# Opening of a pairwise-interaction kernel: gathers, weight preparation and w2 loads in another order, x_pairs in 42 rows a shift

## The reference

```python
h = inputs = e
for i, (W, bias) in enumerate(params):            # W: (200, 1600), (200, 4000), (200, 4000)
    x = einsum('bhd,bmd->bhmd', h, inputs).reshape(B, -1, D)
    y = relu(einsum('oi,bid->bod', W, x) + bias[None, :, None])
    if i != n_layers - 1:
        h, direct = split(y, 2, axis=1)           # 100 maps go on, 100 are output
    else:
        direct = y
    outs.append(direct)
z = concatenate(outs, axis=1).sum(-1)             # (512, 400)
h = concatenate([z, dense_ctx], axis=1)
h = maximum(h @ W_top1 + b_top1, 0.0)
h = maximum(h @ W_top2 + b_top2, 0.0)
y = h @ W_top3
```

## Time and profile before

| | us |
|---|---|
| median of 3 executions (lowest to highest) | 2825.09 (2822.59 to 2827.53) |
| profiled execution, its own time | 2823.11 |
| its span in the profile | 2821.3 |
| TensorE busy (matmul) | 2776.4, 98% |
| VectorE busy | 2637.5, 93% |
| ScalarE busy | 1499.5, 53% |
| GpSimd busy | 851.2, 30% |
| mean granted TensorE clock | 0.997 of full |

### The profile page before, as it was taken

The page is one execution under the profiler, slowest core; times in us unless marked ns, Lnnn a source line. Parts: engine busy times, 40 slices in busy tenths (PEclk is TensorE's granted clock), DMA queues, the critical chain, the costliest instruction groups (busy, mean ns, idle before and its releaser), DMA issues.

```text
span 2821.3 us, 54078 instructions
## 1 busy us (share of the span) xinstructions
PE 2776.4 (98%) x19032; PEld 2760.6 (98%) x19032; DVE 2637.5 (93%) x1945; ACT 1499.5 (53%) x1880; POOL 851.2 (30%) x700
## 2 busy tenths in 40 slices
PE   5899999999999999999999999999999999999999
PEld 5899999999999999999999999999999999999997
DVE  6899999999999999999999999999999999999995
ACT  4555555555555555555555555555555555555553
POOL 5432332332332332323323323323323323333100
PEclk9999999999999999999999999999999999999999
DMA  7333433433433433433334334334334334333330
GB/s 210 85 80 81 93 89 78 96 89 76 101 85 78 98 86 83 95 84 87 92 80 94 88 76 98 89 75 102 85 79 99 85 82 96 84 86 94 85 78 18
DMA packets 286024, 249.66 MB, mean 88 GB/s; under 512 B 31285, under 2 KB 284445, under 8 KB 285892
## 3 DMA queue, kind: packets, MB, share of 16 engines
q1 hardware_dynamic: 216310, 200.56, 25.8%
q0 software_dynamic: 65712, 45.56, 12.3%
q10 hardware_dynamic: 3972, 3.17, 0.4%
HBM read 140.74 MB, written 4.20 MB: 51 GB/s over the span
## 4 chain that ended last, share of the span: by engine, by line
PE 94%; SPq 2%; DMA 1%; issue 1%; POOL 1%; DVE 1%; another core or an unknown queue 0%; ACT 0%; DVEq 0%; ACTq 0%
PE acc L806 62%; PE acc L808 29%; PE hid_ps L819 1%; PE z_ps L823 1%; POOL gathered L445 1%; SPq L380 1%; PE acc L877 0%; DVE product L713 0%; DVE tails L718 0%; SPq L347 0%; SPq L369 0%; DMA hid_rep<-hid 0%; DMA gathered<-in_table,rows_all 0%; PE hid_ps L900 0%
## 5 line engine op out<-in xcount | busy, mean ns | idle before, releaser
L806 PE MATMUL acc<-weights,heads 126*128 126x400 f32 (+1 forms) x9088 | 2690.6, 364 | 12.1 <-DVE tails L718 12.1
L808 PE MATMUL acc<-weights,tails 126*128 126x200 f32 (+1 forms) x9088 | 2320.5, 255 | 0.0
L519 ACT ACTIVATE heads<-product 126x1024 fp32r<-126x1024 f32 (+2 forms) x1152 | 1198.2, 1047 | 1019.9 <-PE acc L808 509.5
L808 PEld LDWEIGHTS acc<-weights,tails 126*128 126x128 f32 (+1 forms) x9088 | 1739.3, 191 | 0.0
L806 PEld LDWEIGHTS acc<-weights,heads 126*128 126x128 f32 (+1 forms) x9088 | 1711.4, 188 | 14.1 <-issue 8.8
L718 DVE TENSOR_TENSOR tails<-product,heads 126x1024 fp32r<-126x1024 f32 (+2 forms) x1152 | 1347.9, 1202 | 1.4 <-ACT heads L519 1.4
L713 DVE TENSOR_TENSOR product<-hid_rep,x_rep 126x2048 f32<-126x2048 f32 x510 | 1166.9, 2288 | 107.1 <-PE acc L808 67.3
L453 POOL DMA_DIRECT2D acc_copy<-acc_copy x189 | 235.0, 1243 | 1726.0 <-ACT acc_copy L525 1724.0
L445 POOL DMA_INDIRECT gathered<-in_table,rows_all x320 | 503.6, 1574 | 101.2 <-issue 97.2
L533 ACT ACTIVATE y_relu<-acc_copy 128x400 f32<-128x400 f32 x192 | 102.4, 533 | 216.6 <-DMA acc_copy<-acc_copy 214.3
L525 ACT ACTIVATE acc_copy<-acc 128x800 f32<-128x800 f32 x192 | 158.6, 826 | 12.7 <-PE acc L808 5.8
(11 more groups left out here) (26 smaller groups left out, 118.1 us busy)
## 6 DMA issues: line engine op xcount, KB each, us to landing
x_rep<-x_rows SPq DMA_DIRECT2D x512, 120.0 KB
hid_rep<-hid SPq DMA_DIRECT2D x511, 120.0 KB
x_pairs<-x_rows SPq DMA_DIRECT2D x191, 280.0 KB
acc_copy<-acc_copy POOLq DMA_DIRECT2D x189, 200.0 KB
hid_rep<-hid SPq DMA_DIRECT2D x511, 5.0 KB
x_pairs<-x_rows SPq DMA_DIRECT2D x63, 120.0 KB
gathered<-in_table,rows_all POOLq DMA_INDIRECT x320
raw_weights<-in_w SPq DMA_DIRECT2D x8, 500.0 KB, 7.4
```

The source lines that it names most:

```text
L519: act.activation(heads[0:rows, ring % HEADS_RING, 0:tiles, :], product[0:rows, ring % PRODUCT_RING, 0:tiles, :], ACT.Copy).then_inc(heads_ ...
L806: nc.tensor.matmul(acc[:, at.parity, c, 0:2 * LAYER], dims(heads[0:rows, ring % HEADS_RING, k, :], c), w, start=(q == 0 and k == 0), stop= ...
L808: last = nc.tensor.matmul(acc[:, at.parity, c, LAYER:2 * LAYER], dims(tails[0:rows, ring % PRODUCT_RING, k, :], c), w[:, 0:LAYER], start=F ...
```

## The change

- `x_pairs` holds 42 rows for each shift where it held 40, so its product part has 126 rows (`ROWS0`), and the row of ones moves from partition 120 to 126. The two rows more hold products with zero weights. All x_pairs loads have 42 or 126 rows.
- VectorE waits for a marker that GpSimd writes after block 0's five gathers, before it adds w0b to w0a.
- The first two chunks of w1 are split ahead of w0. `split_place` maps a chunk to its place in that order, for the waits.
- SP loads the first half of block 0's x_rep right behind block 0's x_pairs, ahead of block 1's x_pairs. The last three chunks of w1, which stood there, go behind block 1's x_pairs. The second half of x_rep goes behind block 0's maps.
- SP loads w2 behind block 1's maps for layer 1, where it stood ahead of them. Its chunks are split three in layer 1 and four in layer 2 of iteration 2, where five were split in layer 0 and 1 up to q = 2 and none in layer 2.
- GpSimd: block 0's repeated maps of group 1 are issued between the stores of blocks 2 and 3, not behind both; block 5's first gather goes ahead of the wait and the `add` before it.
- 4 identity matmuls in place of 9, twice.

```diff
+FIELDS_PADDED = 42
+ROWS0 = SHIFTS * FIELDS_PADDED
-OPERAND_ROWS = (PAIRS0 + 1, PAIRS + 1, PAIRS + 1)
+OPERAND_ROWS = (ROWS0 + 1, PAIRS + 1, PAIRS + 1)
-BUSY = 9
+BUSY = 4
...
             if i == "start":
-                return list(range(split_until[0])) + w1[:4]
+                return w1[:2] + list(range(split_until[0])) + w1[2:4]
             if (i, layer) == (0, 0):
                 return w1[4:]
-            if (i, layer) == (2, 0):
-                return w2[:3]
-            if (i, layer) == (2, 1):
-                return w2[3 + q // 2:4 + q // 2]
+            if (i, layer) == (2, 1) and q > 0:
+                return w2[q // 2 - 1:q // 2]
+            if (i, layer) == (2, 2) and q < GROUPS - 2:
+                return w2[(3, 4, 5)[q // 2]:(4, 5, 7)[q // 2]]
             return []
...
-                parts.append((x_pairs[j:PAIRS0:SHIFTS, 1:1 + TILES0, :],
+                parts.append((x_pairs[j:ROWS0:SHIFTS, 1:1 + TILES0, :],
                               bass.AP(tensor=rows.tensor, offset=rows.offset,
-                                      ap=[[COLS, FIELDS], [SHIFTS * COLS, TILES0], [1, COLS]])))
+                                      ap=[[COLS, FIELDS_PADDED], [SHIFTS * COLS, TILES0], [1, COLS]])))
...
         def _(sp):
-            load_weights(EARLY_LOADS, split_until[1])
+            load_x_rep(0, 0, 0)
             sp.wait_ge(prep_added, 2)
...
                 if not whole and i == 0:
-                    load_x_rep(0, 0, 0)
-                    load_x_rep(0, 0, 1)
+                    load_weights(EARLY_LOADS, split_until[1])
                 if not whole and 0 < i < blocks and l2 is None:
                     for half in range(FLD_HALVES):
                         load_x_rep(duo, parity, half)
-                    load_weights(split_until[1], split_until[2])
...
                     load_hid(0, (0, 2, 3) if not whole and i == 0 else range(HID_OUT))
+                    if not whole and i == 0:
+                        load_x_rep(0, 0, 1)
+                    if not whole and i == 1:
+                        load_weights(split_until[1], split_until[2])
...
         def _(pool):
+                if b == 0:
+                    pool.memset(marker[:, blocks - 1:blocks], 0.0).then_inc(first_rows_asked, 1)
             for b in range(2, FIRST):
                 pool.wait_ge(first_gathered[b], GATHERS)
                 for part in stored_parts(b, b):
                     pool.dma_start(*part).then_inc(first_stored[b], 16)
+                if b == 2:
+                    pool.wait_ge(hid_copied[0], 1)
+                    for part in hid_parts(0, 1):
+                        pool.dma_start(*part).then_inc(hid_first_loaded, 16)
             add(0)
-            pool.wait_ge(hid_copied[0], 1)
-            for part in hid_parts(0, 1):
-                pool.dma_start(*part).then_inc(hid_first_loaded, 16)
...
                 first = 1 + (b - FIRST) * 3
+                ahead = 1 if b == FIRST + 1 else 0
+                for k in range(ahead):
+                    gather(0, k, rows_all[:, b, k:k + 1], x_gathered)
                 add(first)
-                for k in range(FLD_DMA):
+                for k in range(ahead, FLD_DMA):
                     gather(0, k, rows_all[:, b, k:k + 1], x_gathered)
...
         def _(dve):
+            dve.wait_ge(first_rows_asked, 1)
             for n in range(2):
                 dve.wait_ge(prep_loaded[n], 16)
```

23 lines of the change are left out of this document (15 added, 8 removed).

## The result

| | before | after |
|---|---|---|
| median us (runs; lowest to highest) | 2824.6 (22; 2820.9 to 2827.5) | 2828.1 (22; 2826.2 to 2833.9) |
| ratio of the times, 95% interval | | 1.0017 [1.0011, 1.0022] |
| profiled execution, its own time; span | 2823.11; 2821.3 | 2828.56; 2826.8 |
| mean granted clock | 0.997 | 0.996 |

The change costs 0.17%, some 4.8 us by the ratio; by its interval 3.1 to 6.2 (the two medians are 3.5 us apart). 2818.5 was forecast, in 2813.5 to 2825.5: wrong in sign, and outside the range.

A forecast was written before the change was run, and what follows sets the result against it. TensorE, busy for 2776.4 of 2821.3 us, was taken to bound the kernel, with VectorE setting the opening's pace. Terms of -1.1 (w2's tails) and -4.5 (the long gather) took 2824.1 to 2818.5 us, range 2813.5 to 2825.5.

The forecast's parts named there:

- Step 1: Start to block 0's x_pairs: closer gathers save 1.5 us, 42 rows 1.2; block 0's product starts at about 22.7.
- Step 2: w1's load issued 7.1 us later: block 0's accumulator copy +1.7, first layer 1 product +2.0; bounds 0 and +2.9.
- Step 3: w2's loads behind block 1's maps: maps asked for at 64.9, block 1's first layer 1 product at 70.0, -2.4.
- Step 4: w2's tails come later, where VectorE has no hole: +3.3, a closed hole -0.76; TensorE becomes level, -1.1 us.
- Step 5: Block 5's first gather, 11.19 us, issued at about 88 within GpSimd's wait: -4.5 us, bounds 0 and -4.9.
- Rival B: The long gather is not hidden, another behind the same add takes it: 2823.0 us, chance 0.16.
- Step 6: Rows 121 to 127, identity matmuls 9 to 4 twice, block 0's maps on GpSimd and padding: at no cost.
- Rival D: Cold TensorE: with 4 identity matmuls layer 0 of two blocks runs at half clock; 2823.3 us, chance 0.05.
- Rival C: Slower: the long time falls on the add behind the hoisted gather; 2827.4 us, or 2831.9; chance 0.07.

The follow-up runs named there:

- the experiment: The changed kernel with w1's last three loads issued ahead of the first half of x_rep, where they stood before: 2820.17 us, ratio 0.9999 to before.
- the kernel with four memsets: After with w1's load early, five w2 loads waiting for the add, ScalarE's w2 heads one turn earlier, a memset behind each block 0 layer 2 product: 2816.45, 0.9976.
- the kernels with the memset in its place and later: Before plus a one-element VectorE memset, behind block 0's layer 2 product of groups 6 and 7 (2816.79, 0.9974) or behind block 3's layer 0 product (2820.51, 0.9997).

## Why the prediction was wrong, point by point

**Step 1, start to x_pairs.** Product at 24.31, not 22.7. Block 0's gathers did take 0.94 us each but for the first two (1.19 and 1.00), but the x_pairs were asked for 0.9 us earlier and not 1.5. The 42 rows were taken at 1.2 us, near the upper bound; alone they gave 0.12 in one pair of executions, and some 0.5 over all. The Trainium skill (DMA: Bandwidth & Descriptors, "Why a DMA increments its semaphore by 16 and not by 1") would make 1.4 us of it, as the prediction estimated from its rule. The DMA share rises as the rule has it, the time does not fall by as much; why is not shown.

**Step 2, w1's late load. The step that made the change slower.** SP's issue came 6.9 us later, 7.1 was predicted (the five x_rep DMAs took SP 3.8 us, as reckoned, though five times the 0.8 named there are 4.0). But two sizes were off. Behind nine loads from x_rows the weights took 6.1 us to arrive (32.20 to 38.28) where 3.7 had done (25.31 to 29.02): so the last heads came 9.8 us later and not 6.5 to 7.1. And 36.89 was taken as the baseline, which is the late copy of one execution; with the load early the copy is at 34.89. What the step gave as +1.7 to +2.0 was +4.9 against before and +6.9 against what the rest of the change would have had. Its upper bound of 2.9 came from the issue time alone, with no bound for what the load takes from issue to arrival there. In the sum it was worse: the +2.0 was set against VectorE's later gains in step 3 and got no price of its own. By the experiment it is the whole loss against before.

**Step 3, w2's loads behind the maps.** Right. For block 1's first layer 1 product -2.4 was predicted and +0.93 measured (73.31). But the -2.4 held the +2.0 of step 2, so it was -4.4 for w2 alone; the +0.93 hold the +5.8 of the opening, so w2 gave -4.9. From asking for the maps to the product it took 4.7 us (68.66 to 73.31), where about 5 was reckoned (the wait at 93.01 that was named for it, of 0.76 us, does not show that number); only the maps were on hand at 68.3, not 62.9 + 2.0.

**Step 4, w2's tails. The step that used up the forecast gain.** Predicted +3.3 and -0.8 on VectorE and -1.1 for TensorE. On TensorE's account w2 gave -7.0 and then cost 12.0, +5.0 in all. From block 1's first layer 1 product to block 3's layer 0 product VectorE took 38.8 us before and 47.7 in after, +9.0: 3.4 for three more splits (the predicted +3.3), 5.0 for waits, of 5.8 us against 0.8, and 0.5 that was not followed. These waits were not thought of: 2.15 us because the add's DMA, issued behind seven weight loads, took 8.2 us to relu (78.96 to 87.19) where it took 3.6 before (78.02 to 81.64), and 2.3 us in four waits at w2's splits; three of them end with ScalarE's w2 heads, which it makes only behind its other heads of that turn. Both go when five loads wait for the add and ScalarE's heads move up one turn, as the kernel with four memsets shows. "TensorE was 1.1 us behind and will be level" came true only in that TensorE now waits for VectorE, 1.16 us at 106.67, 1.50 at 113.08 and 1.84 at 120.05.

**Step 5, the long gather.** The size was right: 4.9 us at 134.91 to 138.90. The mechanism was not. It was not hidden at 88; it did not occur, and without the hoist it didn't either. So the size was luck: with w2's new arrangement the gather was short where it was, and the hoist had nothing to hide. When a gather that is kept out gets in, depends on VectorE's stream; what keeps it out at all is open. Rival B had the cautious half ("belongs to a moment"), and named no cause. The Trainium skill (SBUF — State Buffer, "SBUF: two separate sides") offers one: VectorE and GpSimd share a pair of ports under an exclusive lock, held for a whole instruction, and a VectorE operation with two inputs in SBUF takes it against a GpSimd operation that reads SBUF. The rows fit that as far as a gather gets in at a seam of VectorE's operations. That it is this lock is argued and not shown, since no run here put operations with one input there. The same page's section "Who interferes with whom" says that such two-input operations did not stall a DMA in its own test; here they did, for 4.5 to 14.6 us, and the measurement decides. And a lock that is held for one instruction does not by itself explain that a gather missed up to eleven seams in a row.

**Step 6.** Right: 4 identity matmuls against 9, and 126 rows, at no cost that can be told (the rows alone were at 0.9990, and block 0's product takes VectorE 2.09 us with 127 rows as with 121). Rival D's half clock came (a granted clock of 0.53 in 38 to 56, where before had 0.85), if for the most part behind the 10.33 us wait, and was absorbed. Rival C did not come: the add was short.

**The account, then.** Against before: the opening with the late w1 load +5.8, w2 -7.0 and +12.0, the gather -4.9: +5.9, where -5.6 was forecast. Of the 11.5 us between them, 5.8 are step 2's, which had no term in the sum, and 6.1 are step 4's, +5.0 where -1.1 stood; the gather gave 0.4 more than its term. Of the sum's two terms only the gather's came in at its size, and not for its reason.

## What to carry over

A load that is moved behind others is late by its issue and by a longer way to its arrival (6.1 and 8.6 us here against 3.7); bound both, and bound the step against what the rest of the change makes of the baseline. Work that fills an engine's wait is only free there: moved, it costs its time and every handshake around it. And where VectorE runs two-input operations without a pause, look for a gather that takes far longer than the rest: a one-element memset beside it gave 0.26%, and one that was over before the gather began, 0.17%. The rearrangement of w2 added nothing to it. Since such a gather comes and goes with small shifts, one kernel's trace does not tell what a change did to it.

## What the hardware did that was not expected

- In 14 of 5440 cases a gather's issue on GpSimd (0.94 us alone) took 4.5 to 14.6 us while VectorE ran two-input operations back to back. It ended 0.94 us after VectorE's first pause or one-element memset, to 0.02 us, in before, in the kernels with the memset in its place and later, and in the changed kernel with the old w2.
- The other 5426 were in by the first seam and took at most 3.1 us, most of those beside VectorE at seams without a pause. What makes a gather miss the first seam, and then up to eleven, is open; it was not tried further.
- A load with a higher DMA share (0.90 against 0.75) ended 0.12 us earlier in one pair of executions and some 0.5 us over all 17, where 1.2 was forecast.
